# A third buffer for the decay factors, and four tap products made three

## The reference, cut to what matters

```python
xz = xn @ W_in
x_br, z = jnp.split(xz, 2, axis=-1)
xc = lax.conv_general_dilated(xc, conv_w, ...)      # four taps, per channel
xb = jax.nn.silu(jnp.transpose(xc, (0, 2, 1)))
delta = jax.nn.softplus(xb @ W_delta + b_delta)
A_bar = jnp.exp(delta[..., None] * A)               # 1024 channels x 16 states
Bx = delta[..., None] * Bm[:, :, None, :] * xb[..., None]
def step(h, inp):
    a_t, bx_t, c_t = inp
    h = a_t * h + bx_t
    return (h, jnp.sum(h * c_t[:, None, :], axis=-1))
```

## Time and profile before

| | us |
|---|---|
| median of 3 runs | 2658.17 |
| lowest and highest of them | 2652.7, 2659.58 |
| the profiled execution | 2653.91 |
| its span, first to last instruction | 2651.9 |
| PE, DVE, ACT, POOL busy | 2309.5, 2265.5, 1669.0, 1728.4 |

### The profile page before, as it was taken

How to read it: one execution, slowest core, us unless ns; L and a number is a source line. 1 busy time by engine, 2 the same in 40 slices (tenths; PEclk the granted TensorE clock), 3 DMA queues, 4 the chain that set the end, 5 groups by cost and what they waited for, 6 DMA issues and landing times. The chain is left out here.

```text
span 2651.9 us, 34212 instructions
## 1 busy us (share of the span) xinstructions
PE 2309.5 (87%) x11520; PEld 1586.2 (60%) x11520; DVE 2265.5 (85%) x2232; ACT 1669.0 (63%) x3332; POOL 1728.4 (65%) x2042
## 2 busy tenths in 40 slices
PE   7778889888898988888988888888888875999997
PEld 5566667676666666757666666666666322444443
DVE  2399999999999999899999999999999835888886
ACT  2567676667667676767676767676766534555554
POOL 0278787878787878778787778787878711222221
PEclk8889999999999999999999999999998987999999
DMA  4102020202010110102020202020104621111110
GB/s 186 72 1 72 9 76 6 76 5 80 16 65 21 61 53 28 65 17 73 9 72 10 72 10 72 10 76 5 72 10 189 233 83 56 60 64 66 59 52 24
DMA packets 48299, 151.74 MB, mean 57 GB/s; under 512 B 8069, under 2 KB 8965, under 8 KB 45198
## 3 DMA queue, kind: packets, MB, share of 16 engines
q1 hardware_dynamic: 48142, 149.76, 15.9%
HBM read 132.37 MB, written 17.37 MB: 56 GB/s over the span
## 5 line engine op out<-in xcount | busy, mean ns | idle before, releaser
L472 POOL TENSOR_TENSOR ring<-ring,Cbc 128x512 f32<-128x512 f32 x1024 | 1283.1, 1275 | 44.5 <-POOL carry L465 0.4
L864 DVE TENSOR_TENSOR_SCAN ring<-a_ps,ring 128x1024 f32<-128x1024 f32 x512 | 1168.0, 2281 | 106.7 <-ACT a_ps L702 105.2
L702 ACT ACTIVATE a_ps<-delta,nA 128x255 f32<-128x255 f32 x2048 | 852.9, 468 | 380.3 <-DVE ring L864 379.4
L1069 PE MATMUL yT_ps<-ident,ring 128*128 128x128 f32 x4096 | 588.1, 284 | 163.5 <-POOL ring L472 160.0
L1069 PEld LDWEIGHTS yT_ps<-ident,ring 128*128 128x128 f32 x4096 | 475.0, 145 | 282.2 <-POOL ring L472 241.9
L856 DVE TENSOR_TENSOR ring<-u_ps,Bbc 128x1024 f32<-128x1024 f32 x512 | 619.7, 1210 | 16.0 <-PE yT_ps L1069 9.3
L1035 PE MATMUL work<-xb,big 128*128 128x256 f32 x2048 | 476.8, 385 | 10.1 <-ACT zs L560 10.1
L1035 PEld LDWEIGHTS work<-xb,big 128*128 128x128 f32 x2048 | 385.5, 193 | 79.5 <-issue 16.9
L465 POOL TENSOR_TENSOR carry<-ring,half 128x4 f32<-128x4 f32 x512 | 127.1, 248 | 361.2 <-DVE ring L864 359.7
L1051 PE MATMUL work<-Wout,xb 128*128 128x512 f32 x512 | 237.7, 599 | 0.0
L1414 POOL TENSOR_TENSOR m<-m,pows 128x1 f32<-128x1 f32 x64 | 34.2, 549 | 311.4 <-DVE m L1546 311.4
(11 more groups left out here) (197 smaller groups left out, 2508.1 us busy)
## 6 DMA issues: line engine op xcount, KB each, us to landing
Bbc<-bc_rows SPq DMA_DIRECT2D x64, 512.0 KB, 4.6
Cbc<-bc_rows SPq DMA_DIRECT2D x64, 512.0 KB, 3.7
xT<-in_xT SPq DMA_DIRECT2D x16, 514.0 KB, 3.5
x_rows<-x2row SPq DMA_DIRECT2D x32, 256.0 KB, 2.0
xp<-x_rows SPq DMA_DIRECT2D x32, 256.0 KB, 2.7
xx<-in_x SPq DMA_DIRECT2D x32, 256.0 KB, 3.0
out_rows<-orow SPq DMA_DIRECT2D x32, 256.0 KB, 2.0
delta<-in_c_w SPq DMA_DIRECT2D x6, 1024.0 KB, 5.3
```

The lines of the kernel that those rows point to most:

```text
L472: nc.gpsimd.tensor_tensor(hp, hp, Cbc[:, G * g + GP * c:G * g + GP * c + GP, :], ALU.mult)\
L702: r = nc.scalar.activation(a_ps[q % 2][:, i, 1:T], delta[:, par, dt, 1:T], ACT.Exp, scale=nA[:, dt, s:s + 1])
L864: dve.tensor_tensor_scan(ring[:, q % RING, :, :].rearrange("p g t -> p (g t)"), a_ps[q % 2][:, :, :].rearrange("p g t -> p (g t)"), ring[: ...
L1069: r = pe.matmul(yT_ps[:, tt, :], ring[:, q % RING, i, P * tt:P * tt + P], ident[:, :], is_transpose=True, start=False, stop=(g == NG - 1 a ...
```

## The change

**Third buffer.** The decay factors rotate over `a_ps[0]`, `a_ps[1]` and a new `a_sb`, by (32k + q) % 3. `a_sb` is in SBUF, in `big[0]`. ACT waits for scan q-3 where it waited for scan q-2. Every third scan, 171 of 512, now reads its factors from SBUF; the others read PSUM as before.

**Three tap products.** Taps 0 and 1 share one matmul over 128 rows: `yp` holds y0 shifted by 0 in rows 0 to 63 and by 1 in rows 64 to 127. The two constant rows of these taps ride in rows 96 and 97 of `y0s` and of the other two products. So a channel tile takes 3 matmuls instead of 4, each over 128 rows where it was 66. In return `y0back` has three more ACT instructions and two more waits of ACT on itself. In step -1 DVE scales 48 smaller pieces where it scaled 32, and clears the unused columns; PE turns 24 tiles of 128 columns where it turned 32 of 66; ACT copies 128x384 where it copied 66x512.

**Places.** `a_sb` occupies piece 6 of `big[0]`, so SP loads that piece of the feed-forward's weights only after the last scan, behind piece 7 on its queue.

```diff
-        Mx = big[0][:, 0:4 * DI].rearrange("p (k c) -> p k c", k=4)
+        Mx = big[0][:, 0:3 * DI].rearrange("p (k c) -> p k c", k=3)
+        yp = big[0][:, 3 * DI:3 * DI + T]
...
-        y0k = big[0][:, 6 * DI:6 * DI + 2 * T].rearrange("p (b t) -> p b t", b=2)
+        y0k = big[0][:, 5 * DI + D:6 * DI].rearrange("p (b t) -> p b t", b=2)
+        a_sb = big[0][:, 6 * DI:7 * DI].rearrange("p (g t) -> p g t", g=G)
...
+        a_of = [a_ps[0], a_ps[1], a_sb]
+        NA = len(a_of)
...
-                        if 2 <= c < 9:
+                        if 2 <= c < 8:
...
                     sp.dma_start(big[0][:, 7 * DI:8 * DI], f_w1[:, 7 * DI:8 * DI]).then_inc(s_big[0], 16)
+                    sp.wait_ge(s_scan, NQ * NBLK)
+                    sp.dma_start(big[0][:, 6 * DI:7 * DI], f_w1[:, 6 * DI:7 * DI]).then_inc(s_big[0], 16)
...
-                    act.wait_ge(s_yh, n + 1)
-                    nc.scalar.activation(y0s[0:NY, fp, 3:T + 3], ps[0:NY, 0:T], ACT.Copy).then_inc(free[BANK["YB"]], 1)
+                    act.wait_ge(s_yh, 2 * n + 1)
+                    nc.scalar.activation(y0s[0:NY, fp, 3:T + 3], ps[0:NY, 0:T], ACT.Copy).then_inc(s_yh, 1)
+                    act.wait_ge(s_yh, 2 * n + 2)
+
+                    nc.scalar.activation(yp[0:N0, :], y0s[0:N0, fp, 0:T], ACT.Copy)
+                    nc.scalar.activation(yp[N0:2 * N0, :], y0s[0:N0, fp, 1:T + 1], ACT.Copy)
+                    nc.scalar.activation(y0s[CROW:CROW + 2, fp, 2:T + 3], y0s[N0:NY, fp, 0:T + 1], ACT.Copy)\
+                        .then_inc(free[BANK["YB"]], 1)
...
-                    wait(act, s_scan, NQ * k + q - 1)
+                    wait(act, s_scan, NQ * k + q - NA + 1)
                     for i in range(G):
                         s = G * g + i
-                        r = nc.scalar.activation(a_ps[q % 2][:, i, 1:T], delta[:, par, dt, 1:T], ACT.Exp,
+                        r = nc.scalar.activation(a_of[(NQ * k + q) % NA][:, i, 1:T], delta[:, par, dt, 1:T], ACT.Exp,
...
+            dve.memset(MTk[:, :, 1:3, NY:P], 0.0).then_inc(s_mtz, 1)
...
-                        for tap in range(4):
-                            r = dve.tensor_scalar(MTk[:, m, tap, :], ps, V[:, V_CW + 4 * m + tap:V_CW + 4 * m + tap + 1],
-                                                  None, ALU.mult)
+                        cw = [V[:, V_CW + 4 * m + tap:V_CW + 4 * m + tap + 1] for tap in range(4)]
+                        for tap in range(2):
+                            dve.tensor_scalar(MTk[:, m, 0, N0 * tap:N0 * tap + N0], ps[:, 0:N0], cw[tap], None, ALU.mult)
+                            dve.tensor_scalar(MTk[:, m, 1 + tap, CROW:CROW + 2], ps[:, N0:NY], cw[tap], None, ALU.mult)
+                            r = dve.tensor_scalar(MTk[:, m, 1 + tap, 0:NY], ps, cw[2 + tap], None, ALU.mult)
...
                     dve.tensor_tensor_scan(ring[:, q % RING, :, :].rearrange("p g t -> p (g t)"),
-                                           a_ps[q % 2][:, :, :].rearrange("p g t -> p (g t)"),
+                                           a_of[(NQ * k + q) % NA][:, :, :].rearrange("p g t -> p (g t)"),
...
-                    for tap in range(4):
-                        r = pe.matmul(ps[:, T * m:T * m + T], Mx[:, tap, c:c + P], y0s[:, fp, tap:tap + T],
-                                      start=(tap == 0), stop=(tap == 3))
+                    for i, rows in enumerate((yp[:, :], y0s[:, fp, 2:T + 2], y0s[:, fp, 3:T + 3])):
+                        r = pe.matmul(ps[:, T * m:T * m + T], Mx[:, i, c:c + P], rows, start=(i == 0), stop=(i == 2))
```

More of the change, by code:

```diff
@@ L33 @@
 NY = N0 + 2
+CROW = 96
 EPS = 1e-5
@@ L156, in scan_phase @@
         WoTg = xdp[:, :, :].rearrange("p a b -> p (a b)")[:, 0:KD * NY].rearrange("p (d n) -> p d n", d=KD)
-        MTk = ring[:, 1:RING, :, :].rearrange("p a b c -> p (a b c)")[:, 0:ND * 4 * NY]\
-            .rearrange("p (m k n) -> p m k n", m=ND, k=4)
+        MTk = ring[:, 1:RING, :, :].rearrange("p a b c -> p (a b c)")[:, 0:ND * 3 * P]\
+            .rearrange("p (m k n) -> p m k n", m=ND, k=3)
         cond = V[:, V_COND:V_COND + 2 * KD].rearrange("p (d b) -> p d b", b=2)
@@ L194, in scan_phase @@
         s_mxs = sem("s_mxs")
+        s_mtz = sem("s_mtz")
         s_mxp = sem("s_mxp")
@@ L550, in mx_copy @@
                         act.wait_ge(s_mxp, m + 1)
-                        nc.scalar.activation(Mx[0:NY, :, P * m:P * m + P],
-                                             abank[2 + m % 2][0:NY, :].rearrange("p (k c) -> p k c", k=4), ACT.Copy)\
+                        nc.scalar.activation(Mx[:, :, P * m:P * m + P],
+                                             abank[2 + m % 2][:, 0:3 * P].rearrange("p (k c) -> p k c", k=3), ACT.Copy)\
                             .then_inc(s_mxc, 1)
@@ L697, in step @@
                         act.wait_ge(s_setD, 8)
-                        act.wait_ge(s_aclr, 3)
-                    wait(act, s_scan, NQ * k + q - 1)
+                        act.wait_ge(s_aclr, 4)
+                    wait(act, s_scan, NQ * k + q - NA + 1)
                     for i in range(G):
                         s = G * g + i
-                        r = nc.scalar.activation(a_ps[q % 2][:, i, 1:T], delta[:, par, dt, 1:T], ACT.Exp,
+                        r = nc.scalar.activation(a_of[(NQ * k + q) % NA][:, i, 1:T], delta[:, par, dt, 1:T], ACT.Exp,
                                                  scale=nA[:, dt, s:s + 1])
@@ L781, in mx_scale @@
                 def mx_scale():
+                    dve.wait_ge(s_mtz, 1)
                     for m in range(ND):
@@ L878, in step @@
                         dve.memset(u_ps[:, :, 0:1], 1.0).then_inc(s_aclr, 1)
+                        dve.memset(a_sb[:, :, 0:1], 0.0).then_inc(s_aclr, 1)
                         dve.wait_ge(s_mxc, ND)
@@ L995, in turn_m @@
                             pe.wait_ge(s_mxc, m - 1)
-                        for tap in range(4):
-                            r = pe.transpose(abank[2 + m % 2][0:NY, P * tap:P * tap + P], MTk[:, m, tap, :], ident[:, :])
+                        for i in range(3):
+                            r = pe.transpose(abank[2 + m % 2][:, P * i:P * i + P], MTk[:, m, i, :], ident[:, :])
                         r.then_inc(s_mxp, 1)
@@ L1015, in z @@
                     tt, c = j // 2, 512 * (j % 2)
-                    pe.matmul(ps[:, :], y0s[:, fp, 3 + P * tt:3 + P * tt + P], Mz[:, c:c + 512],
+                    pe.matmul(ps[:, :], y0s[0:NY, fp, 3 + P * tt:3 + P * tt + P], Mz[0:NY, c:c + 512],
                               start=True, stop=True).then_inc(full[BANK[f"Z{j}"]], 1)
```

## The result

| us | before | changed |
|---|---|---|
| median of 4 runs each | 2656.80 | 2784.12 |
| lowest and highest | 2652.70, 2659.58 | 2783.25, 2789.10 |
| the profiled execution | 2653.91 | 2783.25 |
| PE, DVE, ACT, POOL busy | 2309.5, 2265.5, 1669.0, 1728.4 | 2321.3, 2363.1, 1672.4, 1974.6 |

The changed kernel takes 1.048 times as long (95% interval 1.0465 to 1.0504): 127 us or 4.8% slower, where 2.0% was forecast. The time lies above the forecast's own range (2665 to 2765 us) and just inside the 8-in-10 one (up to 2785). First the groups by line of the changed kernel, which answer to the earlier trace rows: count | busy us, mean ns | idle time before, and what ended it.

What follows compares the result with a forecast made beforehand. DVE was taken to bound the scan phase, POOL becoming as tight with the change. 2653.9 - 100 - 3 + 143 + 32 - 16 = 2710, shifted to 2712 us; own range 2665 to 2765, 8 in 10 2640 to 2785.

Steps and rivals of the forecast that it cites:

- SBUF scans stretched: Scans reading factors from SBUF wait for POOL's instruction in flight: 0.5, 0.46, 0.49 and 0.29 us in slots 2, 5, 8, 11.
- the ledger's 3.35: Layout of DVE and POOL times over 12 slots: 3.35 us lost with the change, 8.9 a step, 143 in 16 steps.
- L835, now L853, less the long ones of before: DVE instruction with two SBUF inputs meets busy POOL in slot 7, 0.65 us; 14 long ones already counted, -16.
- gates and reductions late, and POOL's other work: Gates wait 0.16 and 0.8 us for late POOL; POOL's delta sums and small jobs charged 2 us a step, 32.
- DVE's waits for factors: DVE's scans waiting for ACT's decay factors, 105.2 us; buffer and products would remove 100, ends 80 and 105.
- run-in, end: PE's quarter fewer products before the scans, -3 us; later load of weight piece 6 after the last scan hidden.
- 14 x 1.1: About 14 long L835 records, one a step, counted both in the time before and in the 12-slot layout: -16 us.
- the exclusion: DVE instruction with two SBUF inputs and POOL instruction reading SBUF each hold the other off for a whole instruction.
- rival A: The scan doesn't take part in the exclusion, nothing pays for the gain: 2555 us, faster; chance 0.12.
- the big wait: Slot 17: ACT copies the last tap product, runs Silu with two table loads; scan waits 3.60 us, shrinking to a few tenths.
- small ones: DVE's other waits for decay factors, mostly below 1 us each, which would go.
- Rival D: Pile-up of POOL's other work from slot 28 to 12, gates wait 5 us a step more: 2792 us; chance 0.12.

## Why the prediction was right in direction and wrong in size

The forecast was +56 us on the profiled execution; it came to +129. Term by term:

| term | forecast | measured |
|---|---|---|
| SBUF scans stretched (1.74 of the ledger's 3.35) | 74 | 75 |
| L835, now L853, less the long ones of before | 28 - 16 | 10 |
| gates and reductions late, and POOL's other work | 41 + 32 | 75.5 |
| DVE's waits for factors | -100 | -31.5 |
| run-in, end | -3, 0 | -2.3, 0 |

What the table leaves out nearly cancels: 7.6 us more for `e` and the copy, 8 less for the small layer's exponentials. Of the prediction's sums, 14 x 1.1 is 15.4 and not 16, which changes nothing.

**What held.** A scan takes part in the exclusion as L835 does; rival A falls (`big` scans 2720 ns, one input in PSUM 2279, POOL not reading in the multiply 2334). The price of the exclusion was right in its parts: 0.44 us a scan against 1.74 / 4 = 0.44, L853's mean 1074 instead of 911, 73 us against 75.5 for the late gates and the rest. The last match owes something to luck: that POOL would be busy 96% of a step was too much (111.48 of 131.25 us is 85%), since its halves grew by 0.211 x 1024 / 170 = 1.27 us for each SBUF scan and not by 2.1. In part, I take it, the scans fell where POOL stood waiting for the scan anyway. The end was hidden: the feed-forward's first reader of `big[0]` comes 32.8 us after the last scan, before 32.5.

**The step that failed** is the first of the sum, "I take 100 of the 105.2 us, with 80 and 105 as ends". It is 68 of the 73 us by which the sum is too low. It had three links, and each broke by a measured amount. (1) The products would shrink the big wait "to a few tenths": they shrink it from 3.60 to 1.01 us, and take 39 us in all, alone; this is the only part of the change that pays. (2) With the third buffer the "small ones" would go: they don't, 103.1 us with the buffer alone, and 74.2 or 73.7 with a lead of two or three slots. I read ACT's 379.4 us of waiting for scans as time to spare that a buffer turns into a lead. But ACT can't use the buffer while a copy that waits for PE stands ahead of the factors in its order; with the factors put first, the lead works at once (69.2 to 1.0 us). The row that should have warned me was among those I had read: ACT's 103.7 us for PE's products. (3) PE runs later when POOL is held up, and that gives back some of what the products save. With ACT two slots ahead in both kernels, it waits 98.8 us for the tap products (`xb`) with the SBUF scans and 57.1 without them, and DVE waits 74.2 us for factors instead of 66.2. The 215.9 us of `zs` in the changed kernel are mostly not this, but the lead itself, by which ACT comes earlier to a copy that isn't due; the first line is with POOL only writing, the second with the lead taken back to two slots:

```profile
ACT zs L577 <- PE work L1037: 184.6, 41, 6.4
ACT zs L574 <- PE work L1034: 105.7, 39, 5.5
```

And had the term been right in waits, it would still have been wrong in time: 72.6 us of waits removed are worth 30 us in the changed kernel. The prediction says so itself ("what DVE wins on one side it can't use on the other") and then counts the 100 us in full beside the POOL terms.

**The telltales.** Held: the `big` scans (+0.44), 2.28 from `a_ps`, L853 above 911, 768 products. Missed: 2.1 us for each half (1.97 in the one shown, 1.27 on the mean), the wait for factors below 15 us (73.7), POOL above 120 us a step (111.48 in the one shown), the step (134.7 on the mean, not 129.6). The last sentence of the prediction names the miss: the waits stay, so ACT, not its buffers, was late. Rival D gave nearly the right time, 2792, by a wrong cause: it had the waits for factors gone and POOL never idle.

The Trainium skill (SBUF — State Buffer, "Who interferes with whom") has that a DVE instruction with two SBUF inputs contends with a GpSimd instruction that reads SBUF, and not with one that only writes it. Both halves are borne out for a scan, 2720 against 2334 ns, and what is left in the second number is the ten scans that met a reading instruction. The estimate of 11 us by the Trainium skill (Perfetto Trace Analysis, "Optimizing Scalar/DVE Operations") did not show: with POOL out of the way, SBUF scans run at a median of 2281 ns, PSUM scans at 2280.

## What to carry to other kernels

A spare buffer gives an engine a lead only if nothing that waits for a third engine stands ahead of that work in its order; look at what the engine executes just before the late instruction, and whom that waits for, before counting the wait as the buffer's. Before an operand moves to another memory, look at which neighbour it will then keep out, and be kept out by: here one DVE operand kept in PSUM was worth about 0.9 us each time, of which the stretched record is half (0.44) and the rest is what the neighbour then did late. A wait removed on one of two engines that are both short of time is worth its price only up to the slack of the other: here 30 of 73 us.

## What the runs showed of the hardware that I had not expected

DVE's small `e` instruction, which reads one input from SBUF and a constant (L750 before, L765 now), is stretched too. One group of each, ns min/median/max:

```profile
L750 DVE TENSOR_SCALAR e<-e x16: 257/259/284, 18.3 to 1892.5; 64x256 f32<-64x256 f32 x16
L765 DVE TENSOR_SCALAR e<-e x16: 259/570/1286, 20.5 to 2001.6; 64x256 f32<-64x256 f32 x16
```

With the products alone its median is 259 again (maximum 286). In the steps of the kernel before it always began just ahead of POOL's carry, with no half of the multiply running. In the changed kernel nine of the sixteen begin inside a half, and these take 0.57 to 1.29 us; the others keep 0.26 to 0.28. With POOL only writing all sixteen are at 0.26 to 0.28 again. The copy into `big` goes from 352 to 424 ns on the mean. So not only instructions with two SBUF inputs are held off. The Trainium skill (SBUF — State Buffer, "Who interferes with whom") has that `tensor_scalar` and `copy` can take both ports in a faster mode and then contend. The trace agrees that they contend, by up to 1.03 us an instruction; which mode they ran in no run here shows.

ACT's exponentials take 502 ns on the mean when they write `a_sb` and 469 when they write PSUM.

The granted clock of TensorE, a mean in shares of full speed and so mostly the upper of its two levels (1.2 and 2.4 GHz), is 0.92 in the step shown where it was 0.97, with PE waiting longer for POOL (310.4 us for `ring`, before 160.0) ahead of its turns, whose mean went from 284 to 290 ns. I take it for a consequence and did not test it apart.
